# A graph, state-space and mixture-of-experts layer on one core: bodies written out, and fewer products of tile 1 beside tile 0's front

## The reference, cut to what matters

```python
h  = relu(adj @ layernorm(x) @ gcn_w + gcn_b);  h = layernorm(h) * ln_g + ln_b
xc, z = split(h @ w_in)                       # 256 + 256 columns
u  = silu(conv4(xc) + conv_b)                 # four taps along the rows
dbc = u @ w_xp                                # 8 + 16 (B) + 16 (C) columns
dt = softplus(dbc[:, :8] @ w_dt + b_dt)
# for each of 16 states n, along all 8192 rows:
hst = exp(dt * A[:, n]) * hst + dt * B[:, n] * u;   ys += hst * C[:, n]
x  = x + ((ys + u * D) * silu(z)) @ w_out
# then a mixture of experts on layernorm(x): H = gelu(x @ W1 + b1), softmax over 8 experts,
# the best expert's H @ Wd[e] + bd[e], times its probability, is added to x
```

## Time and profile before

| | |
|---|---|
| timed runs (3) | median 1849.9 us, 1844.93 to 1852.96 |
| profiled execution | 1837.5 us, its span 1835.7 us |
| mean granted clock of TensorE | 0.915 |
| PE busy | 1517.8 us (83%), 4572 instructions |
| DVE busy | 1553.5 us (85%), 2063 |
| ACT busy | 841.8 us (46%), 1494 |
| POOL busy | 865.9 us (47%), 466 |
| DMA | 479.44 MB, mean 261 GB/s |

### The profile page before, as it was taken

How to read it: one execution, slowest core, us unless ns; L and a number is a source line. 1 busy time by engine, 2 the same in 40 slices (tenths; PEclk the granted TensorE clock), 3 DMA queues, 4 the chain that set the end, 5 groups by cost and what they waited for, 6 DMA issues and landing times. The chain is left out here.

```text
span 1835.7 us, 18445 instructions
## 1 busy us (share of the span) xinstructions
PE 1517.8 (83%) x4572; PEld 748.1 (41%) x4572; DVE 1553.5 (85%) x2063; ACT 841.8 (46%) x1494; POOL 865.9 (47%) x466
## 2 busy tenths in 40 slices
PE   6998888989888899898979898989979893633676
PEld 2443233434434444453535443444435342422444
DVE  8017999999998999999899998999899999998621
ACT  3023445454546364546455453636454554634311
POOL 0003443535354464646465554646464645557621
PEclk9999998999998999999999999998999996656788
DMA  8879999979786878878787868787887864333330
GB/s 311 279 251 381 396 393 319 364 280 317 259 302 236 308 269 310 287 274 305 274 289 260 319 235 292 244 316 263 284 292 281 301 230 161 99 131 132 117 75 12
DMA packets 164655, 479.44 MB, mean 261 GB/s; under 512 B 19780, under 2 KB 50512, under 8 KB 164418
## 3 DMA queue, kind: packets, MB, share of 16 engines
q1 hardware_dynamic: 155074, 453.31, 69.9%
q0 software_dynamic: 8320, 20.86, 3.5%
q10 hardware_dynamic: 1152, 4.19, 0.6%
HBM read 448.20 MB, written 33.22 MB: 262 GB/s over the span
## 5 line engine op out<-in xcount | busy, mean ns | idle before, releaser
L1165 PE MATMUL ps_adj<-ring,nodes 128*128 128x512 f32 x2048 | 949.8, 610 | 83.6 <-DMA ring<-adj 55.1
L500 POOL TENSOR_TENSOR h_c<-hidden,bc_ring 128x1024 f32<-128x1024 f32 x256 | 601.0, 2348 | 856.6 <-DVE inject L1031 726.7
L948 DVE TENSOR_TENSOR_SCAN hidden<-decay,state,inject 128x512 f32<-128x512 f32 x512 | 627.3, 1267 | 50.8 <-ACT decay L588 16.8
L1165 PEld LDWEIGHTS ps_adj<-ring,nodes 128*128 128x128 f32 x2048 | 390.6, 196 | 603.2 <-issue 459.0
L588 ACT ACTIVATE decay<-dt_sb,negA 128x512 f32<-128x512 f32 x512 | 339.4, 711 | 2.0 <-issue 1.0
L1031 DVE TENSOR_TENSOR inject<-dtu_sb,bc_ring 128x1024 f32<-128x1024 f32 x256 | 314.1, 1227 | 26.3 <-DMA bc_ring<-bc_dram 19.8
L1001 DVE TENSOR_TENSOR y_sum<-y_sum,h_c 128x1024 f32<-128x1024 f32 x224 | 273.4, 1220 | 26.8 <-POOL h_c L500 25.8
L581 ACT COPY state<-hidden 128x2 f32<-128x2 f32 x255 | 49.2, 193 | 519.5 <-DVE hidden L948 517.3
L465 POOL DMA_INDIRECT out<-o_sb,out_at x68 | 82.1, 1208 | 70.1 <-DVE o_sb L854 57.2
L460 POOL DMA_INDIRECT bins<-rec,dest x60 | 88.7, 1478 | 10.2 <-DVE hidden L948 5.1
L455 POOL DMA_INDIRECT got<-bins,row_at x60 | 84.9, 1415 | 14.6 <-issue 11.5
(11 more groups left out here) (200 smaller groups left out, 1367.9 us busy)
## 6 DMA issues: line engine op xcount, KB each, us to landing
ring<-adj SPq DMA_DIRECT2D x512, 512.0 KB
bc_ring<-bc_dram SPq DMA_DIRECT2D x256, 512.0 KB
wd_ring<-wd_rows SPq DMA_DIRECT2D x64, 320.0 KB
bins<-nodes SPq DMA_DIRECT2D x128, 129.0 KB
nodes<-x_rows ACTq DMA_DIRECT2D x8, 512.0 KB, 12.2
x_tile<-x_rows SPq DMA_DIRECT2D x16, 256.0 KB
wd_rows<-Wd SPq DMA_DIRECT2D x8, 256.0 KB
ring<-Wd SPq DMA_DIRECT2D x1, 2048.0 KB, 7.6
```

What stands on the lines that cost most here:

```text
L500: nc.gpsimd.tensor_tensor(h_c[:, s % 2], hidden[:, s % 2], over_halves(bc_ring[:, s % BC_RING, 1]), ALU.mult).then_inc(hc_ready, 1)
L948: scan = nc.vector.tensor_tensor_scan(hidden[:, s % 2, h], decay[:, s % 2, h], inject[:, h], state[:, h, s:s + 1], ALU.mult, ALU.add)
L1165: last = nc.tensor.matmul(ps_adj[:, 0], nodes[:, m], ring[:, g % RING, m % GROUP], start=(m == 0), stop=(m == J - 1))
```

## The change

The loop is gone: bodies -2 to 15 are all written out, and semaphore values are constants. Which groups of which tile belong to a slot now comes from tables. Body -1 has 13 groups of tile 1 instead of 32; body 0 has the other 19 in slots 0 to 5 (`LEAD`) and 23 of tile 2 from slot 6 on; body 1 has 9 of tile 2 and 26 of tile 3, body 2 has 6 and 28, body 3 has 4 of tile 4 and 32 of tile 5. From body 4 on there are two a slot. `FRONT[i]` gives the slot of each front stage in bodies 0 to 3; in all others stage k is in slot k as before. The store of `rows_sb` is two slots behind the copy stage. The bins are cleared three DMAs a slot from body 1 to body 3, in the order of the rows, with a semaphore for each quarter; the expert rows move to body 3. ACT runs Silu of u ahead of Silu of z in every body.

```diff
+MAIN = {-1: (0, 1, 1, 0, 0, 1, 0, 0, 5, 1, 0, 1, 1, 1, 1, 0),
+        0: (0, 0, 0, 0, 0, 0, 1, 2, 2, 2, 3, 2, 2, 3, 3, 3),
+        1: (0, 0, 0, 2, 2, 2, 2, 2, 2, 2, 2, 2, 2, 2, 2, 2),
+        2: (0, 0, 2, 2, 2, 2, 2, 2, 2, 2, 2, 2, 2, 2, 2, 2),
+        3: (0, 3, 2, 2, 2, 2, 2, 2, 2, 2, 2, 2, 2, 2, 2, 3)}
+LEAD = {0: (4, 3, 3, 3, 3, 3), 1: (4, 3, 2), 2: (3, 3), 3: (4,)}
+FRONT = {0: (6, 6, 7, 7, 8, 8, 9, 10, 11, 12, 12, 13, 14, 15, 15, 15),
+         1: (2, 2, 3, 3, 4, 5, 6, 7, 8, 9, 10, 11, 12, 13, 14, 15),
+         2: (2, 2, 3, 3, 4, 5, 6, 7, 8, 9, 10, 11, 12, 13, 14, 15),
+         3: (1, 1, 2, 3, 4, 5, 6, 7, 8, 9, 10, 11, 12, 13, 14, 15)}
...
         def bodies(eng, body):
-            for i in range(-2, 6):
+            for i in range(-2, TILES):
                 body(i, i % 2, **stages(i))
-            with eng.Fori(6, TILES - 3, 2) as i:
-                body(i, 0, **ALL)
-                body(i + 1, 1, **ALL)
-            for i in range(TILES - 2, TILES):
-                body(i, i % 2, **stages(i))
...
+        def groups_at(i, s):
+
+            found, tile = [], i + 1
+            for table in (LEAD, MAIN):
+                counts = table.get(i, () if table is LEAD else (2,) * SLOTS)
+                if 0 <= tile < TILES and counts:
+                    first = GROUPS - sum(counts) if table is LEAD else 0
+                    at = first + sum(counts[:s])
+                    found += [(tile, g) for g in range(at, at + (counts[s] if s < len(counts) else 0))]
+                tile += 1
+            return found
...
-                for g in range(GROUPS):
-                    if adjacency:
-                        src = adj[bass.ds(i + 2, 1), g].rearrange("a p c n -> p (a c) n")
-                        used = c.value(adj_used, 2, g - RING + 1)
-                        dma = sp.dma_start(ring[:, g % RING], src)
-                        if used is not None:
+                for s in range(SLOTS):
+                    for tile, g in groups_at(i, s):
+                        dma = sp.dma_start(ring[:, g % RING], adj[tile, g])
+                        used = tile * GROUPS + g - RING + 1
+                        if used > 0:
                             dma.wait_op(adj_used, used, "sem-ge")
                         dma.then_inc(ring_in[g % RING], 16)
-                        if isinstance(i, int) and i in (0, 1):
-                            if (i, g) == (0, 0):
-                                sp.wait_ge(node_ready, 8)
-                            for n in range(2):
-                                clear_bins((2 * i + n) * GROUPS + g)
-                        if isinstance(i, int) and i == 2 and g % 4 == 0:
-                            expert_row(g // 4)
+                    if i in (1, 2, 3):
+                        for n in range(3 * (SLOTS * (i - 1) + s), min(3 * (SLOTS * (i - 1) + s + 1), FILLS)):
+                            clear_bins(n)
+                    if i == 3 and s % 2 == 0:
+                        expert_row(s // 2)
...
-                    if g == 23 and front:
+                    if s == min(f[9] + 2, SLOTS - 1) and front:
                         sp.dma_start(bc_dram.ap()[q].rearrange("s h n -> h s n"), rows_sb[:]
...
-                    if front and s == 8:
+                    if front and s == f[8]:
+                        c.wait(conv_step, 1, 2 * (TAPS - 1))
+                        nc.scalar.activation(u_sb[:], u_sb[:], ACT.Silu).then_inc(u_ready, 1)
                         c.wait(xz_ready, 1, 4)
                         nc.scalar.activation(z_sb[:, q], z_sb[:, q], ACT.Silu)
-                        c.wait(conv_step, 1, 2 * (TAPS - 1))
-                        nc.scalar.activation(u_sb[:], u_sb[:], ACT.Silu).then_inc(u_ready, 1)
```

More of the change, by code:

```diff
@@ L370, in body @@
                 q = 1 - p
-                if isinstance(i, int) and i == TILES - 2:
+                f = FRONT.get(i, range(SLOTS))
+                if i == TILES - 2:
                     sp.wait_ge(adj_used, GROUPS * TILES)
@@ L395, in body @@
+                    if s == 7 and batch:
                         sp.wait_ge(table_in, 16 * 2 * EXPERTS)
-                        if freed_ is not None:
-                            sp.wait_ge(by_done, freed_)
-                        sp.wait_ge(ctrl_step, chosen_)
+                        c.wait(by_done, -6, PICKS)
+                        c.wait(ctrl_step, -4, 13)
                         load_experts(wd_ring[:, p], p, wd_in[p])
-                    if g == 23 and front:
+                    if s == min(f[9] + 2, SLOTS - 1) and front:
@@ L415, in body @@
-                    if g == GROUPS - 2 and mamba:
+                    for d, t in next_state(s, mamba, front):
+                        freed = c.value(hc_ready, d, t - BC_RING + 1)
+                        if t == 0:
+                            c.wait(rows_out, d, 16)
+                        dma = sp.dma_start(bc_ring[:, t % BC_RING],
+                                           bc_dram.ap()[p if d == 0 else q, t:t + 1].broadcast_to([P, 2, T]))
+                        if freed is not None:
+                            dma.wait_op(hc_ready, freed, "sem-ge")
+                        dma.then_inc(bc_in[t % BC_RING], 16)
@@ L472, in body @@
                 fast = ffn and not front
-                for per in (1, 4, 5, 6, 13, 16, 64):
-                    c.times_of(per)
                 for s in range(SLOTS):
@@ L593, in body @@
                     keep_state(s)
-                    if front and s == 0:
+                    if front and s == f[0]:
                         c.wait(adj_used, 1, GROUPS)
@@ L643, in body @@
                                                  ).then_inc(conv_first, 1)
-                    if front and s == 7:
+                    if front and s == f[7]:
                         c.wait(y_ready, -1, 1)
@@ L675, in body @@
                         nc.scalar.copy(bt_sb[:], ps_e[:, 0]).then_inc(bt_ready, 1)
-                    if front and s == 12:
+                    if front and s == f[12]:
                         for h in range(2):
@@ L1019, in body @@
                         finish(c, -4, p, got[:, p], ps_e[:, 1])
-                    if front and s == 15:
+                    if front and s == f[15]:
                         c.wait(inject_ready, 0, SLOTS)
@@ L1188, in body @@
                         token_columns(q)
-                    if front and s in (5, 6):
+                    if front and s == f[5]:
                         c.wait(hn_ready, 1, 1)
                         for k in range(2):
-                            if s == 6:
-                                c.wait(xz_ready, 1, k + 1)
-                            product(ps_f[:, k], [(win_sb[:, 2 * (s - 5) + k], front_a[:])]).then_inc(xz_done, 1)
+                            product(ps_f[:, k], [(win_sb[:, k], front_a[:])]).then_inc(xz_done, 1)
+                    if front and s == f[6]:
+                        for k in range(2):
+                            c.wait(xz_ready, 1, k + 1)
+                            product(ps_f[:, k], [(win_sb[:, 2 + k], front_a[:])]).then_inc(xz_done, 1)
                     if ffn and s == 7:
@@ L1206, in body @@
                                 ).then_inc(dbc_done, 1)
-                    if front and s == 9:
+                    if front and s == f[9]:
                         c.wait(low_ready, 1, 1)
@@ L1218, in body @@
                         transpose(got[:, p], ps_e[:, 0])
-                    if front and s == 10:
+                    if front and s == f[10]:
                         c.wait(rows_ready, 1, 1)
```

120 lines of the change are left out of this document (49 added, 71 removed).

## The result

| | before | after |
|---|---|---|
| timed on one chip (20 runs each) | median 1847.18 us, 1834.35 to 1856.72 | median 1853.95 us, 1845.31 to 1865.21 |
| profiled execution | 1837.5 us, span 1835.7 | 1856.9 us, span 1855.1 |
| mean granted clock | 0.915 | 0.902 |

The ratio is 1.0048, with a 95% interval of 1.0029 to 1.0066. The change makes the kernel slower by about half a per cent; 1825.9 was forecast, with a range of 1808 to 1845.

What follows compares the result with a forecast made beforehand. VectorE was taken as the bound from the first scan at 144.28 us on. Terms -32.3 + 2 + 1 - 10.2 + 3.8 + 11.7 = -24.0 took the median 1849.9 to 1825.9 us, range 1808 to 1845.

Steps and rivals of the forecast that it cites:

- A: Tile 0's front with 26 products of tile 1 beside it instead of 64: first scan at 112.0, -32.3 us.
- B: The 19 groups taken out come back in bodies 0 to 3 and fit: +2 us for body 0, +1 for 1 to 3.
- C: Bodies 6 to 13 without the loop: three back-edge waits go, -10.2 us; bodies like straight 4 and 5, +3.8.
- D: Silu of u before z: Gelu and wxp 1.06 us later in eleven bodies with a batch, +11.7 us.
- rival 2: In the bodies with a batch, the Silu table load comes late too: 14.1 us more, 1840; chance 0.10.
- rival 1: The Silu order costs nothing: -35.7 us, 1814; chance 0.17.
- E: Clock during tile 0's front: PE pauses stay under 1 us, so 0; up to 15 us if it fell to 1.2 GHz.
- Rival 4: PE becomes the bound of bodies 0 to 3, which grow by all 32.7 us of products: +8.3, 1858; chance 0.10.
- rival 3: Straight code stalls in its own fetches, or body 0 starves of broadcasts at its tail: some 10 us, 1836; chance 0.08.
- point of decision: The fourth rival decides once bodies 0 to 3 grow by more than 27 us together.

Runs made afterwards that it cites:

- x4: The changed kernel with eight ring places instead of four for tiles 0 to 4; ratio 0.9831 to the kernel before.
- x6: The changed kernel with the clears four a slot in bodies 0 and 1, as before, instead of three in 1 to 3; ratio 1.0123 to the kernel before.
- x8: x5 with the expert rows written in slots 8 to 15 of body 0 instead of body 3; ratio 0.9782 to the kernel before.
- x1: The kernel before with its loop written out and nothing else; ratio 0.9923 to the kernel before.
- x12: x1 run once more, as the anchor on the chip of x9; ratio 0.9916 to the kernel before.
- x2: x1 with Silu of u ahead of Silu of z; ratio 0.9976 to the kernel before.
- x3: The changed kernel with Silu of z ahead of Silu of u again; ratio 0.9951 to the kernel before.
- x7: The changed kernel with each slot's broadcast issued ahead of its ring loads in bodies 0 to 3; ratio 1.0085 to the kernel before.
- x9: x1 with eight ring places for tiles 0 to 4, products, front and clears left where they were; ratio 0.9879 to the kernel before.
- x5: x4 with Silu of z ahead of Silu of u again; ratio 0.9812 to the kernel before.

## Why the prediction was wrong

**A, the earlier start (-32.3): right.** The chain came stage by stage as walked: copy 75.10, first `win` 84.31, `wxp` 96.68 (97.4 forecast), store issued 99.20 (100.0), `dtu` done 106.85 (108.1), first scan 109.67 (112.0). The path over DRAM does bind, by the 1.47 us that `inject` waits. Store and broadcast were put at 3.6 and 7.1 us; from the store's issue to the broadcast's it is 4.0, and from there to `inject` 5.1. These rows of the kernel after answer and the earlier trace rows:

```profile
99.20 0.73 SPq L399 DMA_DIRECT2D bc_dram<-rows_sb  x1
...
103.20 0.33 SPq L406 DMA_DIRECT2D bc_ring<-bc_dram  x1
```

```profile
105.63 1.22 DVE L1023 TENSOR_TENSOR dtu_sb<-dt_sb,u_sb 128x1024 f32<-128x1024 f32 x1
108.33 1.23 DVE L1030 TENSOR_TENSOR inject<-dtu_sb,bc_ring 128x1024 f32<-128x1024 f32 x1 [1.47 <-DMA bc_ring<-bc_dram]
```

**B, the groups come back (+2 and +1): the step that failed.** It measured +49.5. I compared PE's need of a body (81.7 of 90 us) and its DMA bytes with the body's length; both fit, and x4 shows that they nearly do (380.9 us for 365.4). What I took for "keep the pace that body 0 shows now" was a slot's need, 5.16 us of PE and 5.3 of DMA, as if loads could be issued at will. But a load is issued only when a place is free, and I had the number for its return in the earlier trace rows, 7.13 us for the same 512 KB, and used it only in part A. With it, four places and one group's use of 1.72 us give a group every 2.2 us, so 42 us for nineteen groups where body 0 of before needs 32.9; the trace shows 39.7. On top come the broadcasts behind ring loads on SP and the late sum in front of decay on ACT. x4, with eight places, takes 34 us of the 49.5 away.

The terms that I put at nothing in the same part had a price too. Of clears and expert rows I said that they cost nothing, by the rows of a body with two groups a slot: x6 shows 17 us for putting the clears closer and earlier, x8 9 us for taking the rows out of body 3 beside clears. The front stages pushed together are the likely cause of a few us of waits for decay that stay with eight places; no run isolates them.

The Trainium skill, "DMA: Bandwidth & Descriptors", Anatomy of one DMA, fits a single DMA issued from GpSimd as 2.0 us and its bytes at 436 GB/s; for 512 KB that would be an estimated 3.2 us. The loads here are issued from SP, with up to four ring loads and a broadcast under way, and took 5.7 to 7.3 us to their use, about twice that: a fit for a DMA alone doesn't give the depth that a ring needs.

**C, no loop (-10.2 + 3.8): right.** The three stalls are gone. Straight bodies 6 to 13 are 98.7 us each in x1 and 99.1 in x12, for the 99.3 that bodies 4 and 5 suggested, so the +3.8 measured -0.8 and +2.3, low but within its bounds of -2 to +5. The rule of "Runtime: NRT & Kernel Launch", Instruction fetch mechanics, in the Trainium skill, that a taken branch out of the held pages stops the engine, agrees with x1's three rows and with the packets counted above: the waits of 3.1 to 4.1 us and the 6 or 7 packets are gone with the branches.

**D, the Silu order (+11.7): right,** with `wxp` 1.0 us later in each of eleven bodies and 10 and 18 us in the timed pairs. That the gain of the loop and this loss are of one size is chance. In body 8 of the kernel after, answering:

```profile
972.33 1.06 ACT L653 ACTIVATE u_sb<-u_sb 128x1024 f32<-128x1024 f32 x1 [2.94 <-DVE u_sb L1009]
973.29 1.04 ACT L655 ACTIVATE z_sb<-z_sb 128x1024 f32<-128x1024 f32 x1
```

```profile
976.47 3.62 PE L1097 MATMUL ps_f<-u_sb,wxp_sb 128*128 128x512 f32 x4 [4.74 <-ACT H L659]
```

The table load of Silu runs at 968.10, ahead of the wait, so rival 2 is out; the timed pairs speak against rival 1. PE's wait before `wxp` is 4.74 us for 3.05.

**E, the clock (0): right for the start,** where the granted clock stayed 1.00 with pauses of 0.4 to 0.8 us. In the later bodies it may be part of D's price, below; the mean over the span fell from 0.915 to 0.902. The window from the copy of tile 0's sum to the first scan:

```profile
75.04:109.67 34.63, 32.92 (x74) 13.56 (x75) 10.17 (x14) 17.78 (x26) 0.00 (x0) 1.00 0.62 214
```

**The rivals.** Rival 4 gave the right side and nearly the right time (1858), but not for its reason. Its +8.3 beside the 6.8 measured is luck. It charged 32.7 us of products, with PE full; measured are 49.5, with PE waiting 47.6 us for data, and x4 takes 34 back with the same products. Its point of decision held: the bodies grew by more than 27 us, and the gain was gone. Of rival 3's two causes, the fetches of straight code don't show in x1, and the broadcasts that body 0 lacks are those of its first slots, not of its tail.

The sum with measured terms, in the profiled executions: -34.6 + 49.5 + 1.3 + 2.0 + 1.2 = +19.4; in bodies 4 to 13 the loop's -11 and the order's +12 cancel.

**What stays open.** The written-out loop gains 15 us in the timed runs and 10.7 and 8.3 in the spans of its two profiled executions. That is no riddle: the profiled execution of before is 10 us below its median, theirs are 3 and 2 below. In x1, x12, x2, x3 and after, `inject` waits 2.5 to 4.7 us in body 1's slot 13, though x1, x12 and x2 have two groups a slot there. Its broadcast was issued only 5.8 to 7.0 us ahead. In before it was 6.4, and DVE came to it as it landed, 0.3 us early; in all kernels with eight places, and in x7 with its other order, it is 13.9 us and there is no wait. So this too is a broadcast behind ring loads. Why SP comes to it later in x1 than in before, with the same instructions, I can't say. Of the 15.5 us by which x4's bodies 0 to 3 are longer than before's, body 3 has 10; x8 takes some 9 of them back. Whether the rest is more than the 5 us between like kernels isn't shown.

## What to carry to other kernels

Before piling more work into a slot, ask of each stream: places of its buffer, divided by the time from a load's issue to the end of its use. Sums over a long stretch, busy share or bytes, can't show that. Where work is moved to be nearer its neighbours, deepen the buffer in the same step: here either edit alone was worth +0.3 or -0.4 points, both within noise, the two together -1.1 (x1 to x3, x9 and x5). What is free beside a light load need not be beside a heavy one: clears and rows cost little each alone in body 3 and 9 us together. A change of several edits should be priced edit by edit, since a small one (an order of two activations, half a per cent) can eat what another gives.

## What the hardware showed beyond expectation

The DMA engines' busy share doesn't tell how near they are to their limit. Body 1 has a share of 0.98 at 321 GB/s after, 1.02 at 356 in x4, and body 0 of before 1.04 at 394: shares near one were read at rates 23% apart. And x4 moved the same groups, broadcasts and clears in 34 us less, from shares of 0.89 to 0.99.

A pause of PE can cost twice. In body 10 of the kernel after it waits 4.93 us before `wxp`; the windows show a granted clock of 0.50, that is 1.2 GHz, behind it, 1.00 again, and then 0.56 and 0.50 during the logits and after, though the windows have PE busy all the time there (with its modelled ends, so short waits between products can be in it). The timeline of PE, then the windows:

```profile
1175.38 3.75 PE L1097 MATMUL ps_f<-u_sb,wxp_sb 128*128 128x512 f32 x4 [4.93 <-ACT H L659]
...
1190.32 5.81 PE L1097 MATMUL ps_y<-wg_sb,H 128*128 128x8 f32 x32
```

```profile
1176.00:1181.00 5.00, 5.00 (x7) 2.02 (x6) 4.08 (x5) 4.25 (x8) 4.26 (x3) 0.50 0.45 150
1186.00:1191.00 5.00, 5.00 (x16) 2.11 (x15) 4.91 (x6) 3.08 (x6) 2.75 (x2) 1.00 0.79 283
1191.00:1196.00 5.00, 5.00 (x29) 5.00 (x28) 4.91 (x6) 0.00 (x0) 2.41 (x2) 0.56 0.56 213
1196.00:1201.00 5.00, 5.00 (x7) 2.14 (x8) 3.38 (x6) 2.85 (x4) 3.79 (x3) 0.50 0.04 13
```

The 32 logit products (128x8) take 5.81 us there, 5.80 in body 4 and 3.77 in body 8. Scan 13 then waits 6.0 us in body 10 and 5.9 in body 4, where it waits 2.0 to 2.8 in seven of the other eight. What makes the clock fall the second time no run isolates.
